# Score products of a decoder layer on half of the array's rows, and the first two of them side by side

## The reference

```python
Q = _split(query @ W_q.T)
K = _split(key @ W_k.T)
V = _split(value @ W_v.T)
scores = jnp.einsum('bhqd,bhkd->bhqk', Q, K) / jnp.sqrt(jnp.float32(D_K))
scores = jnp.where(mask, -jnp.inf, scores)
attn_w = jax.nn.softmax(scores, axis=-1)
```

## Time and profile before

| | |
|---|---|
| median of 3 runs | 537.59 us (537.46 to 537.86) |
| time of the profiled execution | 541.87 us |
| its span | 540.1 us |
| TensorE busy | 501.5 us, 93% |
| VectorE busy | 374.5 us, 69% |
| ScalarE busy | 251.0 us, 46% |
| GpSimd busy | 260.0 us, 48% |
| score products | 128 records of 422 to 880 ns, median 425 |
| mask products | 64 records, median 296 ns |

### The profile page before, as it was taken

How to read it: one execution, slowest core, us unless ns; L and a number is a source line. 1 busy time by engine, 2 the same in 40 slices (tenths; PEclk the granted TensorE clock), 3 DMA queues, 4 the chain that set the end, 5 groups by cost and what they waited for, 6 DMA issues and landing times.

```text
span 540.1 us, 10882 instructions
## 1 busy us (share of the span) xinstructions
PE 501.5 (93%) x3286; PEld 450.1 (83%) x3286; DVE 374.5 (69%) x1114; ACT 251.0 (46%) x835; POOL 260.0 (48%) x369
## 2 busy tenths in 40 slices
PE   6789999989999869988999999999999999999991
PEld 5657888878888757878799999999999999999980
DVE  3767979858677886537977667665667656766774
ACT  3436666756666436653244334344443334444320
POOL 4534222212212240418267666665676756766565
PEclk9879999999999979999999999999999999999997
DMA  8109930835575625406546666666666665666420
GB/s 231 12 4 302 348 113 6 273 112 180 176 234 172 198 74 210 152 21 229 183 127 214 220 225 206 202 192 194 211 220 227 217 208 202 203 215 231 143 51 1
DMA packets 57280, 93.69 MB, mean 173 GB/s; under 512 B 12018, under 2 KB 49017, under 8 KB 52103
## 3 DMA queue, kind: packets, MB, share of 16 engines
q1 hardware_dynamic: 49975, 79.91, 44.3%
q0 software_dynamic: 5616, 12.82, 7.8%
q10 hardware_dynamic: 1632, 0.27, 0.3%
HBM read 65.64 MB, written 30.18 MB: 177 GB/s over the span
## 4 chain that ended last, share of the span: by engine, by line
PE 35%; issue 19%; POOL 19%; DVE 16%; DMA 7%; ACT 2%; POOLq 1%; ACTq 0%; SPq 0%; DVEq 0%
PE psum_b L1495 8%; PE psum_v L1628 6%; PE psum_a L1594 6%; DMA work<-weighed_outputs,routing 4%; POOL routing L772 4%; POOL out L776 4%; POOL work L768 3%; POOL work L763 3%; PE psum_m L1646 2%; POOL front_then_w_ring L729 2%; DMA weighed_outputs<-work 2%; PE psum_m L1495 2%; DVE routing L1364 2%; PE psum_c L1615 2%; PE psum_a L1739 1%
## 5 line engine op out<-in xcount | busy, mean ns | idle before, releaser
L969 ACT ACTIVATE front_then_w_ring<-psum_a,front_then_w_ring 128x128 f32<-128x128 f32 x160 | 45.8, 369 | 73.3 <-PE psum_a L1739 73.3
L879 ACT ACTIVATE work<-psum_a,score_max 128x77 f32<-128x77 f32 x256 | 62.4, 335 | 34.4 <-DVE score_max L1136 34.3
L1739 PEld LDWEIGHTS psum_a<-front_then_w_ring 128*128 128x128 f32 x640 | 74.4, 192 | 3.9 <-issue 3.0
L1739 PE MATMUL psum_a<-front_then_w_ring 128*128 128x128 f32 x640 | 75.1, 275 | 2.6 <-ACT front_then_w_ring L959 2.0
L969 ACT ACTIVATE front_then_w_ring<-psum_b,front_then_w_ring 128x128 f32<-128x128 f32 x152 | 43.3, 369 | 69.1 <-PE psum_b L1739 69.1
L1762 PE MATMUL psum_v<-expert_w,front_then_w_ring 128*128 x320 | 72.7, 380 | 0.1
L1739 PEld LDWEIGHTS psum_b<-front_then_w_ring 128*128 128x128 f32 x608 | 70.9, 192 | 0.9
L1739 PE MATMUL psum_b<-front_then_w_ring 128*128 128x128 f32 x608 | 71.1, 275 | 0.0
L1762 PE MATMUL psum_c<-expert_w,front_then_w_ring 128*128 x304 | 68.8, 379 | 0.0
L1762 PEld LDWEIGHTS psum_v<-expert_w,front_then_w_ring 128*128 128x128 f32 x320 | 59.3, 190 | 7.6 <-issue 0.4
L1762 PEld LDWEIGHTS psum_c<-expert_w,front_then_w_ring 128*128 128x128 f32 x304 | 56.3, 190 | 6.9
(11 more groups left out here) (242 smaller groups left out, 887.9 us busy)
## 6 DMA issues: line engine op xcount, KB each, us to landing
front_then_w_ring<-in_w1b SPq DMA_DIRECT2D x39, 1028.0 KB, 4.9
weighed_outputs<-routing SPq DMA_DIRECT2D x16, 1024.0 KB, 6.6
expert_w<-in_w SPq DMA_DIRECT2D x8, 1024.0 KB, 10.3
weighed_outputs<-work SPq DMA_DIRECT2D x37, 128.0 KB, 2.3
token_rows<-front_then_w_ring SPq DMA_DIRECT2D x16, 128.0 KB, 1.8
second_buffers<-in_x SPq DMA_DIRECT2D x4, 256.0 KB, 4.9
token_rows<-routing SPq DMA_DIRECT2D x1, 1024.0 KB, 5.4
front_weights_then_tail<-in_b SPq DMA_DIRECT2D x1, 1024.0 KB, 8.4
```

Source lines behind the costliest of these rows:

```text
L879: last = act.activation(prob[:, u % RING_U, at_k:at_k + SC], pa[:, H % 2, g * SC:(g + 1) * SC], ACT.Exp, bias=smax[:, j % 2, head:head + 1])
L969: last = act.activation(hidT[t % 2][:, c, :], src[:, n, q * P:(q + 1) * P], ACT.Gelu, bias=bias[:, c:c + 1])
L1739: last = pe.matmul(dst[:, n, q * P:(q + 1) * P], w1[:, k, c * P:(c + 1) * P], xtT[t % 2][:, k, :], start=(k == 0), stop=(k == KD - 1))
```

## The change

The score product takes only the 64 rows of its four heads, from both operands. It is split from the mask product, and in the loop both still follow each other. Ahead of the loop the two products come first, and both masks after them. The rows left out were multiplied by zero.

```diff
             def scores(H):
+                score_products(H)
+                add_mask(H)
+
+            def add_mask(H):
+                it, h = divmod(H, STEPS)
+                dst = pa[:, H % 2, 0:HG * SC]
+                at_q = (it % CPB) * CHUNK + h // QUADS * P
+                pe.matmul(dst, mask_b[0:SC, at_q:at_q + P], eye4[0:SC, :, :].rearrange("p h k -> p (h k)"),
+                          start=False, stop=True).then_inc(s_mm, 1)
+
+            def score_products(H):
                 it, h = divmod(H, STEPS)
                 j, quad = divmod(h, QUADS)
                 half, g = divmod(quad, HC // HG)
...
                 dst = pa[:, H % 2, 0:HG * SC]
-                pe.matmul(dst, qT[it % 2][:, half, j * P:(j + 1) * P],
-                          kbd[:, it // CPB, half, g * HG:(g + 1) * HG, :].rearrange("p h k -> p (h k)"), start=True, stop=False)
-                at_q = (it % CPB) * CHUNK + j * P
-                pe.matmul(dst, mask_b[0:SC, at_q:at_q + P], eye4[0:SC, :, :].rearrange("p h k -> p (h k)"),
-                          start=False, stop=True).then_inc(s_mm, 1)
+                rows = slice(g * HG * DK, (g + 1) * HG * DK)
+                pe.matmul(dst, qT[it % 2][rows, half, j * P:(j + 1) * P],
+                          kbd[rows, it // CPB, half, g * HG:(g + 1) * HG, :].rearrange("p h k -> p (h k)"), start=True, stop=False)
...
-            scores(0)
-            scores(1)
+            score_products(0)
+            score_products(1)
+            add_mask(0)
+            add_mask(1)
             keys(2)
```

## The result

The change makes the kernel slower: 553.6 us (550.43 to 556.16, 4 runs) against 537.53 us (536.79 to 537.86, 4 runs), a ratio of 1.0298 with a 95% interval from 1.0242 to 1.0355. That is 16.1 us, where 6.1 were forecast.

What follows compares the result with a forecast made beforehand. TensorE was taken to bound most of the loop; +6.5 us for the loop, +0.1 and -0.5 for the prologue gave +6.1 us on 537.59, so 543.7 us, range 536.2 to 555.5.

Steps and rivals of the forecast that it cites:

- The bound and the streaming: Loop: TensorE bounds most stretches; a 64-row product streams no faster, two passes of 0.26 us as now, nothing gained.
- rival (E): Loop: the product of half the rows streams in half the time, 14 us less, 523 us; chance 0.01.
- rival (F): The array isn't divided, the smaller operand is treated as 128 rows, nothing overlaps, 537.6 us; chance 0.04.
- The step that failed: Loop: each change between 128 and 64 rows costs 0.06 us, an uncovered load; two a step over 54 steps, 6.5 us.
- (B): The forecast itself: 0.02 to 0.12 us for each change of division, 2 to 13 us more; chance 0.38.
- (C): The array is emptied each time, 0.16 to 0.22 us a change, 554.5 to 561 us; chance 0.17.
- The prediction's own signs: Loop: distances before the product and after its second pass each 0.06 us longer; prologue: second product starts under first's second pass.
- 54 steps at full price: Loop: 54 of 62 products lie in TensorE's own stretches, each paying two changes of 0.06 us, 6.5 us in all.
- the 8 steps that I had counted as covered: Loop steps in VectorE's stretches, whose longer TensorE work is hidden; without that cover they would add 1.0 us.
- The prologue: Ahead of the loop: one of four passes overlaps, 0.5 us gained at the lower clock; the way back costs about 0.1 us.
- (A): Changes of division are free and one pass of the prologue is hidden, 537.1 us; chance 0.28.
- (D): Changes free, prologue's second product wholly hidden (-1.03 us), a stretch at clock 0.50 missed (-1.1 us), 535.5 us; chance 0.12.

Runs made afterwards that it cites:

- the 96 rows: Changed kernel with 96 rows instead of 64 in half of the loop's products, 128 in the others, prologue as before: 539.85 us, ratio 1.0006 to the kernel before.
- the loop alone: Changed kernel with 64 rows in the loop's 62 products only, prologue as before the change: 552.19 us, ratio 1.0219 to the kernel before.
- the change again: The changed kernel with no edit, run once more beside the kernel before on the same chip: 553.8 us, ratio 1.0249.

## Why the prediction was wrong

**The bound and the streaming: right.** TensorE sets the pace of the loop, a pass on 64 or 96 rows streams as long as one on 128 (0.26 us), and rival (E) is out. The change does divide the array: four passes take the time of two, so rival (F) is out too.

**The step that failed** is "I take 0.06 us, since the row of the same transposes after a wait is the nearest to a matmul that finds nothing prepared". The two changes of a step were put at 0.12 us together, and are 0.29 us. Two things were wrong in it. First, I took the uncovered load alone and left out the gap between the matmul ahead and that load, though I had its bound (0.16 us, from the tail of a record). It costs 0.09 us, on the way in and on the way out, with a transpose, a mask or a product ahead, and 0.07 us behind L1570. Second, the load had the wrong row. Transposes load faster than products of 32 bits (the trace of before records 0.14 us for L1615's loads and 0.19 for the product's). A row of the right kind was in the trace of before, the key projection after a wait and without one:

```profile
33.65 1.99 PE L1495 MATMUL psum_m<-front_then_w_ring,front_weights_then_tail 128*128 128x256 f32 x8 [0.71 <-ACT front_then_w_ring L844]
...
47.64 1.89 PE L1495 MATMUL psum_m<-front_then_w_ring,front_weights_then_tail 128*128 128x256 f32 x8
```

It gives 0.10 us, and 0.10 us is what the product's load costs in the changed kernel. On the way out I charged the same load again, where the mask's 16-bit load costs 0.006 us. With the right terms a step is 2 x 0.09 + 0.10 + 0.01 = 0.29 us, which lies between (B) and (C). The prediction's own signs missed part of it: the two distances that it named grew by 0.09 us each, and the load's 0.10 us sits in a third, from the first pass to the second, which it expected to stay.

The Trainium skill, TensorEngine Tiling (Array Packing), section Key Properties, says that a change of the tiling mode drains TensorE. The trace agrees so far as it shows a gap of 0.09 us at each change; the 96 rows, which pay nothing, fit it as well. I named the rule and then priced the step by a row that holds no such change.

**54 steps at full price: a little too many.** 54 x 0.293 = 15.8 us; the loop alone measured 9.9 to 13.7, the change again 11.1 to 15.8 with the prologue's gain in it, its first runs 13.0 to 19.1. The prediction said that the product's weight load is hidden now. For 14 of the 62 products it wasn't, and these lose only 0.194 us; in four more steps a wait of 0.11 us behind the mask is filled. Over 62 steps that is 44 x 0.293 + 14 x 0.194 + 4 x 0.184 = 16.4 us more of TensorE's work, and 14.2 us of it in the 54 steps that I had counted.

From the first turn of exponentials to the first matmul of the experts the profiles have 192.3 us before and 204.7 after, 12.4 us more. TensorE's records leave 11.0 us of that stretch empty before and 9.5 after: the longer steps fill 1.6 us of waits, for instance the one for ScalarE's exponentials at the end of VectorE's first stretch, 1.42 us before and 0.83 after. That is a little less than the 8 steps that I had counted as covered amount to (2.1 us). In the profile of before another 3.4 us of the stretch are at the lower clock, which is 1.7 us that the profile after doesn't have. That gives 16.4 - 1.6 - 1.7 = 13.1 us against the 12.4 found. The loop alone, by the same sum, gives 16.4 - 2.8 - 1.6 = 12.0 us, and its profile has 12.1.

**The prologue: the way wrong, and the size right only at the other clock.** I had 0.5 less 0.1 us, from one hidden pass of four at the lower clock and a way back. Two passes are hidden: the records begin in twos, two within 0.01 us of each other and the other two 0.36 us later, and since the two passes of one product lie 0.36 us apart everywhere else, each two are of different products. The 0.42 us measured at the upper clock match my 0.4 by luck; at the lower one, for which I had made the sum, it is about 0.75 us. The reasoning that a pass of product 1 must wait behind the second pass of product 0 is refuted. It drew on the Trainium skill's TensorE: Matmul & The Clock Gate, Part 3, that matmuls start and end in program order: for whole products the trace doesn't contradict that, but the two passes of a 32-bit product don't hold up the product behind it.

**The rivals.** (A) and (D) fall with the 293 ns of a step. (C)'s 0.16 to 0.22 us a change holds for the way in (0.09 + 0.10 = 0.19 us), and not for the way out (0.10 us). Of (D) the half about the second product wholly hidden is true.

## What to carry to other kernels

Before a matmul is cut to half of the array's rows, look at what stands ahead of it and behind it: if those use more than 64 rows, as here, each change leaves a gap (0.09 us here) and uncovers a load (0.10 us for 32-bit weights, almost nothing for 16-bit ones), and the smaller matmul itself is no shorter. Here it paid only where two matmuls on different halves, and in different banks, stood next to each other; then the second one is free. A pair of two-pass products gained 0.42 us in the prologue, where the array was idle ahead of it, and 0.23 us by its distances in the loop. Moving matmuls in order to make such pairs can cost far more than they give, if it takes away the lead over the engines that empty the banks.

## What was not expected of the hardware

Two 32-bit products on different halves of the array run pass beside pass: four passes of 308 columns in 0.72 us, when one product's two take 0.71. And the time of an execution depends more on the granted clock than the first runs let see. In profiles of kernels with the same prologue as before, TensorE is at 0.50 for 6.8 to 13.7 us ahead of the loop and for 7.2 to 10.3 us in it. In the nine profiles with the changed order it is 3.4 to 6.8 us ahead of the loop; yet the two of these kernels whose loop is that of before took the time of before. The 51 later runs of the kernel before spread from 536.8 to 543.0 us, where its first four lay within 1.1 us. The seven of them with a mean granted clock of 0.984 or more took 536.8 to 539.9 us, the thirteen with 0.972 or less 540.7 to 542.5. The prediction held a change of 1.08 us for one that can be told; the intervals of the experiments are 2.5 us to either side at their widest, and 1.3 at their narrowest. That is why a gain of 0.4 us had to be read from the trace.
